# Three rooms and two score banks in PSUM for three attention stages, with q, k and x turned split as they leave PSUM

## The chip, the cores and the metric

One core of one Trainium2 chip runs the whole program. The time is that of the device, in microseconds, and lower is better. The engines are TensorE (PE in the rows; PEld are its weight loads), VectorE (DVE), ScalarE (ACT), GpSimd (POOL) and SyncE (SP), which issues most transfers. SBUF is the memory of 128 partitions from which the engines work; PSUM, into which TensorE writes, has 8 banks of 128 x 512 floats.

## The reference

Eight layers are added to x (8 samples of 256 tokens, width 256) one after the other, each scaled by a gate. The change touches three attentions, with 16 heads of width 16:

```python
# l1x: cross attention on ctx_768, masked queries attend to all keys alike
q = x @ Wq.T; k, v = y @ Wkv.T
attn = softmax(where(pad_mask, (q * scale) @ k, -1e9)); out = attn @ v
...
# l3x: cross attention with biases and a clip
q = query @ Wq + bq; k = key_value @ Wk + bk; v = key_value @ Wv + bv
attn = softmax(clip(q @ k * scale, -CLAMP, CLAMP)); out = (attn @ v) @ Wo + bo
...
# l3f: self attention under two key masks; five register tokens see both
qkv = x @ W_qkv; x_pos, x_neg = masked_attn(pos), masked_attn(~pos)
out = concatenate([(x_pos[:REG] + x_neg[:REG]) * 0.5, where(pos, x_pos, x_neg)]) @ W_proj + b_proj
```

x enters each layer normalized. The other layers are a similarity, a feed-forward layer, two mixtures of experts and an attention of another kind.

## The kernel before

The program is written engine by engine; each engine runs its list in order and waits on semaphores. Nine phases follow each other: l0x, l0f, l1x, l1f, l2x, l2f, l3x, sim, l3f. l1x, l3x and l3f are instances of `Packed` and run through the functions `packing`, one for each engine. This order is written out by hand: a loop over n (a sample) and in it over the 16 heads h, in which `if h == ...` places the other work of samples n − 1 to n + 3.

Products of q, k, v and their inputs are taken in three passes over a high and a low part of each operand (`mm3`). For this each tensor is split: high is the value rounded to the fast format, low the rest. Before, xT (x normalized and transposed) and k are copied out of PSUM by ScalarE (`turned`, `keys`, into xt and kf), q by VectorE (`queries`, into qf, with mask or bias), and then GpSimd makes both parts (`parts`: a cast, L719, and a subtraction, L721). SyncE copies the parts of q and k into qpack and kpack (L572), so that a head's scores are one matmul of 48 rows.

For each head TensorE makes the scores (`scores`, L2012), VectorE takes their negated maximum (`maximum`, L1080), and TensorE makes them a second time, transposed and with the maximum folded in as two more rows (`scores_turned`, L2029); ScalarE writes the exponential (L1619), in l3x VectorE clips it (L1172), and `values` multiplies it by v (L2044). The maxima of 8 heads are turned by TensorE (m0 and m1, L1998) and go into qpack by a transfer. The outputs are turned (z0 and z1, L2054), divided by their sums on VectorE (L1152 and L1159), in l1x added to x (L903), in l3x and l3f turned again ("on", L2066 to L2071) and projected ("y", L2079). l3f has beside this attention of its registers: us, ut and up (L2088, L2096, L2104).

PSUM: scores use the banks 0, 1 and 5 in turn, the transposed ones 2 and 3, the values 4. All else takes two rooms, the banks 6 and 7, in turn, in an order that `Packed` lists. TensorE waits before each use until the use two before it has been released:

```python
def room(self, what, n):
    b = sum(self.used) % 2
    self.place[what, n] = b, self.used[b]
...
if i >= 3:
    pe.wait_ge(m["mx"], at["mx"] + i - 2)
```

## Time and profile before

| | |
|---|---|
| median of three runs | 2746.6 us (2744.47 to 2755.7) |
| profiled execution: time, span | 2744.37 us, 2742.6 us |
| mean granted TensorE clock, share of full | 0.827 |
| PE, DVE, ACT, POOL busy | 77%, 47%, 27%, 33% of the span |
| l1x, l3x, l3f | about 264 to 502, 2082 to 2361, 2435 to 2735 us |

An engine's busy time is the union of its instructions. A wait is idle time just before an instruction, put down to what released it last. The granted clock is a share of 2.4 GHz, where 0.5 is 1.2 GHz. A room's release is seen only through what released it: TensorE at L1998 waiting for "DVE x L903" is m0 waiting for a room that the addition to x frees.

### The profile page before, as it was taken

Reading aid. Unit: us, or ns where it says so; the run is one execution under the profiler, and the core shown is the slowest. Engines: PE = TensorE matmul, PEld = TensorE weight load, DVE = VectorE, ACT = ScalarE, POOL = GpSimd, SP = SyncE. Lnnn points to the kernel's source line nnn. Section 1 sums busy time; section 2 is a strip of 40 time slices with the busy share of each in tenths; the row PEclk is TensorE's granted clock in tenths of the full one; section 3 lists DMA queues with packets and bytes.
Section 4 is the critical chain, followed back from the end, with each engine's and each line's share of the span. In section 5 each row is a group of like instructions: output and inputs, shape, how many; then the busy total and the mean of one; then the engine's idle time right before and its main releaser. Section 6 shows DMA issues by size and latency. Waiting matters only on the chain.

```text
span 2742.6 us, 32575 instructions
## 1 busy us (share of the span) xinstructions
PE 2110.3 (77%) x11634; PEld 1555.5 (57%) x11634; DVE 1292.8 (47%) x2652; ACT 729.5 (27%) x1621; POOL 896.9 (33%) x822
## 2 busy tenths in 40 slices
PE   3597888529999981788988899569953988549887
PEld 3476655427777771455655566458842655335554
DVE  2444566525454442233334334535534798445554
ACT  1121245202221110223332333112310344112344
...
GB/s 128 156 162 5 86 75 49 66 92 104 125 115 96 123 81 106 63 4 3 3 0 3 3 3 0 6 71 107 202 80 81 59 67 35 0 26 61 49 50 45
DMA packets 120208, 177.73 MB, mean 65 GB/s; under 512 B 10900, under 2 KB 105172, under 8 KB 117460
## 3 DMA queue, kind: packets, MB, share of 16 engines
...
q14 instruction: 49, 0.40, 0.1%
...
## 4 chain that ended last, share of the span: by engine, by line
PE 52%; issue 18%; DVE 11%; POOL 8%; DMA 5%; ACT 3%; SPq 1%; another core or an unknown queue 1%; DVEq 0%; POOLq 0%; ACTq 0%
PE bank L1735 8%; PE bank L1736 6%; PE bank L1737 6%; PE bank L1859 5%; PE bank L2012 4%; PE bank L1838 4%; PE bank L2044 4%; DMA ew<-in_we 3%; POOL ewl L773 3%; PE bank L1872 3%; PE bank L1886 3%; DVE nmf L1080 2%; PE bank L1849 2%; DVE x L1356 1%; POOL ewh L771 1%
## 5 line engine op out<-in xcount | busy, mean ns | idle before, releaser
L1080 DVE TENSOR_REDUCE nmf<-bank 128x2 f32<-128x512 f32 x384 | 258.9, 688 | 200.8 <-PE bank L2012 199.3
L1619 ACT ACTIVATE pT<-bank 128x512 f32<-128x512 f32 x384 | 223.2, 597 | 350.5 <-PE bank L2029 348.9
L1328 DVE TENSOR_TENSOR bank<-sil,bank 128x512 f32<-128x512 f32 x136 | 94.8, 697 | 312.7 <-ACT sil L1669 300.6
L1735 PE MATMUL bank<-split,ewl 128*128 128x512 f32 x514 | 213.4, 415 | 34.1 <-POOL ewl L773 17.3
L2012 PE MATMUL bank<-kpack,qpack 48*128 48x256 f32 (+1 forms) x768 | 201.6, 372 | 25.6 <-DMA qpack<-qhl 15.6
L2029 PE MATMUL bank<-qpack,kpack 50*128 50x256 f32 (+1 forms) x768 | 201.6, 364 | 12.7 <-ACT pT L1619 12.7
L773 POOL TENSOR_TENSOR ewl<-ew,ewh 128x1536 fp32r<-128x1536 f32 (+1 forms) x47 | 205.9, 4381 | 3.8
L1736 PE MATMUL bank<-split,ewh 128*128 128x512 f32 x514 | 204.5, 398 | 0.0
L1737 PE MATMUL bank<-split,ewh 128*128 128x512 f32 x514 | 204.3, 397 | 0.0
L771 POOL CAST ewh<-ew 128x1536 fp32r<-128x1536 f32 (+1 forms) x47 | 85.3, 1814 | 354.6 <-DMA ew<-in_we 343.9
L1002 DVE TENSOR_REDUCE nmax<-bank 128x2 f32<-128x512 f32 x128 | 87.6, 690 | 233.4 <-PE bank L1859 230.1
L838 POOL TENSOR_TENSOR esum<-esum,minus 128x2 f32<-128x2 f32 x128 | 89.8, 702 | 327.6 <-ACT arena L1528 327.5
L2012 PEld LDWEIGHTS bank<-kpack,qpack 48*128 48x128 f32 (+1 forms) x768 | 130.8, 226 | 110.0 <-issue 49.8
L1528 ACT ACTIVATE arena<-bank,nmax 128x256 f32<-128x256 f32 x256 | 118.9, 470 | 248.1 <-DVE nmax L1002 246.0
L1735 PE MATMUL bank<-ewh,split 128*128 128x256 f32 x544 | 168.1, 309 | 19.6 <-DVE split L1331 13.1
L1669 ACT ACTIVATE sil<-bank 128x512 f32<-128x512 f32 x136 | 81.3, 598 | 352.4 <-PE bank L1737 319.5
L1462 ACT ACTIVATE arena<-bank 128x512 f32<-128x512 f32 x154 | 91.9, 597 | 300.4 <-PE bank L1838 112.6
L1859 PE MATMUL bank<-arena 64*128 64x256 f32 x512 | 155.9, 447 | 6.2 <-ACT arena L1462 6.2
L1736 PE MATMUL bank<-ewl,split 128*128 128x256 f32 x544 | 156.7, 288 | 0.0
L1737 PE MATMUL bank<-ewh,split 128*128 128x256 f32 x544 | 156.1, 287 | 0.0
L2029 PEld LDWEIGHTS bank<-qpack,kpack 50*128 50x128 f32 (+1 forms) x768 | 127.1, 216 | 29.8 <-ACT pT L1619 18.9
L1735 PEld LDWEIGHTS bank<-split,ewl 128*128 128x128 f32 x514 | 98.4, 191 | 73.9 <-DVE split L1331 21.0
...
## 6 DMA issues: line engine op xcount, KB each, us to landing
...
```

The lines of the kernel that those rows point to most:

```text
L771: nc.gpsimd.tensor_copy(high, whole).then_inc(m["wh"], 1)
L773: nc.gpsimd.tensor_tensor(low, whole, high, ALU.subtract).then_inc(m["ws"], 1)
L1080: V.tensor_reduce(nmf[:, c, :, j, r], bank[(0, 1, 5)[i % 3]][:, :].rearrange("p (t k) -> p t k", t=T), AXX, ALU.max, negate=True).then_inc ...
L1528: ins = A(prob[h % 3][:, t * S:(t + 1) * S], bank[h % 3][:, t * S:(t + 1) * S], ACT.Exp, bias=nmax[:, h, t:t + 1], accum_out=esum[:, h, t: ...
L1619: A(pT16[i % 8][:, :], bank[2 + h % 2][:, :], ACT.Exp, scale=s.qscale).then_inc(m["e"], 1)
L1735: mm(out_, al, bh, start=start, stop=False)
L1736: mm(out_, ah, bl, start=False, stop=False)
L1737: return mm(out_, ah, bh, start=False, stop=stop)
L1838: ins = mm(dst, w[:, c, gr * P:(gr + 1) * P], of[:, c, :], start=c == 0, stop=c == kt_ - 1)
L1859: ins = mm(bank[h % 3][:, t * S:(t + 1) * S], qT[0][r0:r0 + 64, gr, t * P:(t + 1) * P], kT[r0:r0 + 64, gr, :], start=True, stop=True)
L2012: ins = mm(bank[(0, 1, 5)[i % 3]][:, t * S:(t + 1) * S], q[rows, r, t * P:(t + 1) * P], k[rows, r, :], start=True, stop=True)
L2029: ins = mm(bank[2 + h % 2][:, t * S:(t + 1) * S], k[rows, r, t * P:(t + 1) * P], q[rows, r, :], start=True, stop=True)
```

## The change

The three stages get three rooms (banks 5, 6 and 7) and two score banks (0 and 1). The high part of xT, k and q is now written by ScalarE straight out of PSUM, with the bias where there is one (`high_part`, `turned`), and the low part by VectorE, which subtracts the high part from the same bank and then frees the room by a memset that waits for the subtraction (`low_part`). GpSimd keeps the split of the context and the power for the norm. q has two split buffers. In l1x the mask is a factor on rstd in place of one on q, and the two halves of a sample are added to x in one operation. In l3x the bias of v is multiplied by wo once and added to the output's bias. The register scores of l3f take the split parts in three passes. Several pieces of work move by one to four heads.

```diff
+        self.banks, self.rooms = (0, 1), (5, 6, 7)
...
-        self.place, self.used = {}, [0, 0]
+        self.place, self.used = {}, [0 for _ in self.rooms]
...
+        if bias:
+            self.room("bt", 0)
+            self.room("by", 0)
         for n in range(-3, B + 1):
-            for what, at, there in (("us", n + 2, own), ("m1", n, True), ("v", n + 2, True), ("xT", n + 3, True),
-                                    ("ut", n + 2, own), ("z0", n - 1, True), ("z1", n - 1, True), ("up", n + 2, own),
+            for what, at, there in (("us", n + 2, own), ("m1", n, True), ("v", n + 2, True), ("ut", n + 2, own),
+                                    ("z0", n - 1, True), ("z1", n - 1, True), ("xT", n + 3, True), ("up", n + 2, own),
                                     ("m0", n + 1, True), ("on", n - 1, self.proj), ("k", n + 3, True),
                                     ("q", n + 3, True), ("y", n - 1, self.proj)):
...
-        b = sum(self.used) % 2
+        b = sum(self.used) % len(self.rooms)
...
+                        sp.wait_ge(m["ks"], at["ks"] + p + 1)
+                        rows_of(0, kpack[p % 3], khl, (0, 0, 1), m[f"kl{p % 3}"])
...
+                        sp.wait_ge(m["qs"], at["qs"] + p + 1)
                         for j in range(2):
-                            rows_of(p, j, qpack[p % 3], qhl, (0, 1, 0))
+                            rows_of(j, qpack[p % 3], qhl[p % 2], (0, 1, 0), m[f"pl{p % 3}"])
...
-                def parts(dst, src, done, k):
-                    nc.gpsimd.tensor_copy(dst[:, 0, :, :], src).then_inc(m[done], 1)
-                    pool.wait_ge(m[done], at[done] + 2 * k + 1)
-                    nc.gpsimd.tensor_tensor(dst[:, 1, :, :], src, dst[:, 0, :, :], ALU.subtract).then_inc(m[done], 1)
...
-                                used("q", p - 1)
-                                used("v" if s.own else "q", p - 1)
-                            parts(xT16, xt[:, :, :], "xs", p)
...
-                            filled("k", p)
-                            if p > 0:
-                                sent(p - 1)
-                            parts(khl, kf[:, :, :], "ks", p)
...
+                    if p < B and not s.own:
+                        pool.wait_ge(m["ct"], at["ct"] + 16 * p + 16)
+                        if p > 0:
+                            used("v", p - 1)
+                        nc.gpsimd.tensor_copy(cT16[:, 0, :, :], ct[:, :, :]).then_inc(m["cs"], 1)
+                        pool.wait_ge(m["cs"], at["cs"] + 2 * p + 1)
+                        nc.gpsimd.tensor_tensor(cT16[:, 1, :, :], ct[:, :, :], cT16[:, 0, :, :], ALU.subtract)\
+                            .then_inc(m["cs"], 1)
+                    if p + 1 < B:
+                        root({"asked": asked[s.name]}, p + 2, rstd[:, :], rstd[:, :], mhalf[:, 0:T])
...
+                    if s.mask:
+                        ch.link(tt(rstd[:, :], rstd[:, :], maskf[:, n * T:(n + 1) * T], ALU.mult))
...
+                def low_part(what, n, hl, bias=None):
+
...
+                    dve.wait_ge(m[sent], at[sent] + n + 1)
+                    if what == "xT":
+                        if n > 0:
+                            made("q", n - 1)
+                            made("v" if s.own else "q", n - 1)
+                    elif what == "k" and n > 0:
+                        dve.wait_ge(m[f"kl{(n - 1) % 3}"], at[f"kl{(n - 1) % 3}"] + 96 * ((n - 1) // 3 + 1))
+                    elif what == "q" and n > 1:
+                        dve.wait_ge(m[f"pl{(n - 2) % 3}"], at[f"pl{(n - 2) % 3}"] + s.packs * ((n - 2) // 3 + 1))
+                    if what == "k" and s.own and n > 0:
+                        made("us", n - 1)
...
+                    if what == "q" and s.own:
...
+                        ch.link(tt(whole, src[:, :, 0:NREG].rearrange("p j (r o) -> p j r o", o=1).broadcast_to(four),
+                                   hm[:, :, :].rearrange("p j (o h) -> p j o h", o=1).broadcast_to(four), ALU.mult))
+                        ch.link(V.tensor_copy(qx[:, 0, :, :], qxf[:, :, :]))
+                        tt(qx[:, 1, :, :], qxf[:, :, :], qx[:, 0, :, :], ALU.subtract).then_inc(m["ux"], 1)
+                    high, low = hl[:, 0, :, :], hl[:, 1, :, :]
+                    if bias is None:
+                        tt(low, src, high, ALU.subtract).then_inc(m[parts], 1)
...
+                        for j in range(2):
+                            ins = stt(low[:, j, :], src[:, j, :], bias[:, j:j + 1], high[:, j, :], ALU.add, ALU.subtract)
+                        ins.then_inc(m[parts], 1)
+                    dve.wait_ge(m[parts], at[parts] + n + 1)
+                    V.memset(idle[:, 1:2], 0.0).then_inc(done, 1)
...
+                        tt(both[:, t * D:(t + 1) * D].rearrange("p (h e) -> p h e", h=NH), z4[:, :, 0:16], scale, ALU.mult)\
+                            .then_inc(done, 1)
+                        if t == T - 1:
+                            for u in range(T):
+                                b, k = s.place[f"z{u}", n]
+                                dve.wait_ge(m[f"mf{b}"], at[f"mf{b}"] + k + 1)
+                            ch.link(stt(x[:, n * T:(n + 1) * T, :], both[:, :].rearrange("p (t d) -> p t d", t=T), gate,
+                                        x[:, n * T:(n + 1) * T, :], ALU.mult, ALU.add))
...
+                        if h == 0 and 0 <= n + 2 < B:
+                            low_part("q", n + 2, qhl[n % 2], bq3 if s.bias else None)
...
-                        if h == 5 and s.bias and 0 <= n + 2 < B:
-                            values(n + 2)
...
-                        if h in (7, 8) and 0 <= n - 1 < B:
-                            outputs(n - 1, h - 7)
...
+                        if h == 6 and 0 <= n - 1 < B:
+                            outputs(n - 1, 0)
+                        if h == 8 and 0 <= n - 1 < B:
+                            outputs(n - 1, 1)
+                        if h == 9 and n + 3 < B:
+                            low_part("xT", n + 3, xT16)
...
+                        if h == 13 and n + 3 < B:
+                            low_part("k", n + 3, khl, bk3 if s.bias else None)
...
-                        if h == 14 and n + 3 < B:
-                            queries(n + 3)
-                            if s.own:
-                                register_queries(n + 3)
...
+                    from_, _ = made("xT", n)
...
-                    copy(xt[:, :, :], halves(from_)).then_inc(done, 1)
...
+                    copy(xT16[:, 0, :, :], halves(from_)).then_inc(m["xh"], 1)
...
+                        act.wait_ge(m[f"kl{(n - 1) % 3}"], at[f"kl{(n - 1) % 3}"] + 96 * ((n - 1) // 3 + 1))
+                    if what == "q" and n > 1:
+                        act.wait_ge(m[f"pl{(n - 2) % 3}"], at[f"pl{(n - 2) % 3}"] + s.packs * ((n - 2) // 3 + 1))
+                    if bias is None:
+                        ins = copy(hl[:, 0, :, :], halves(from_))
+                    else:
                         for j in range(2):
-                            ins = A(kf[:, j, :], from_[:, j * S:(j + 1) * S], ACT.Identity, bias=bk3[:, j:j + 1])
...
-                    ins.then_inc(done, 1)
+                            ins = A(hl[:, 0, j, :], from_[:, j * S:(j + 1) * S], ACT.Identity, bias=bias[:, j:j + 1])
+                    ins.then_inc(m[what + "h"], 1)
...
-                        if h == 6 and n + 3 < B:
-                            turned(n + 3)
...
+                        if h == 9 and n + 3 < B:
+                            turned(n + 3)
...
-                        if h == 12 and n + 3 < B:
-                            keys(n + 3)
+                        if h == 13 and n + 3 < B:
+                            high_part("k", n + 3, khl, bk3 if s.bias else None)
+                        if h == 15 and n + 3 < B:
+                            high_part("q", n + 3, qhl[(n + 3) % 2], bq3 if s.bias else None)
...
-                    if i >= 3:
-                        pe.wait_ge(m["mx"], at["mx"] + i - 2)
+                    if i >= len(s.banks):
+                        pe.wait_ge(m["mx"], at["mx"] + i + 1 - len(s.banks))
...
-                        mm(to[0:NX, 0:S], qx[:, j, :], kf[:, j, :], start=j == 0, stop=False)
+                        mm3(to[0:NX, 0:S], [qx[:, w, j, :] for w in range(2)], [khl[:, w, j, :] for w in range(2)], j == 0, False)
...
-                        if h == 0 and s.own and 0 <= n + 2 < B:
+                        if h == 0 and s.proj and 0 <= n - 2:
+                            projected(n - 2, 1)
...
-                        if h == 5 and n + 3 < B:
+                        if h == 4 and s.own and 0 <= n + 2 < B:
+                            register_turned(n + 2)
+                        if h == 5 and 0 <= n - 1:
+                            outputs(n - 1, 0)
+                        if h in (6, 10, 14) and 0 <= n < B:
+                            values(n, h // 4 - 1)
+                        if h == 7 and 0 <= n - 1:
+                            outputs(n - 1, 1)
+                        if h == 8 and n + 3 < B:
                             turned(n + 3)
...
-                            outputs(n - 1, h - 6)
-                        if h in (5 + s.late, 9 + s.late, 13 + s.late) and 0 <= n < B:
-                            values(n, h // 4 - 1)
...
-                        if h == 9 and 0 <= n + 1 < B:
+                        if h == 10 and 0 <= n + 1 < B:
                             maxima(n + 1, 0)
...
-                        if h in (10, 11) and n + 3 < B:
-                            keys(n + 3, h - 10)
-                        if h in (12, 13) and n + 3 < B:
-                            queries(n + 3, h - 12)
-                        if h in (14, 15) and s.proj and 0 <= n - 1:
-                            projected(n - 1, h - 14)
+                        if h in (11, 12) and n + 3 < B:
+                            keys(n + 3, h - 11)
+                        if h in (13, 14) and n + 3 < B:
+                            queries(n + 3, h - 13)
```

What stands on TensorE in l1x, for a sample in the middle of the stage, from the first turning of outputs (L2054) on. L2012 are scores, L2029 the transposed ones; the names show the banks. Before:

```order
L2012 MATMUL bank0<-kpack0,qpack0 128x256 x2
L2029 MATMUL bank2<-qpack2,kpack2 128x256 x2
L2054 MATMUL bank7<-ident,oT16 128x128 x4
L2012 MATMUL bank1<-kpack0,qpack0 128x256 x2
L2029 MATMUL bank3<-qpack2,kpack2 128x256 x2
L2054 MATMUL bank6<-ident,oT16 128x128 x4
L2012 MATMUL bank5<-kpack0,qpack0 128x256 x2
L2029 MATMUL bank2<-qpack2,kpack2 128x256 x2
L2012 MATMUL bank0<-kpack0,qpack0 128x256 x2
L2029 MATMUL bank3<-qpack2,kpack2 128x256 x2
```

And in the changed kernel, where L2016, L2033, L2058 and L1967 are scores, transposed scores, outputs turned and x turned:

```order
L2016 MATMUL bank1<-kpack0,qpack0 128x256 x2
L2033 MATMUL bank3<-qpack2,kpack2 128x256 x2
L2058 MATMUL bank7<-ident,oT16 128x128 x4
L2016 MATMUL bank0<-kpack0,qpack0 128x256 x2
L2033 MATMUL bank2<-qpack2,kpack2 128x256 x2
L1967 MATMUL bank5<-ident,xn 128x128 x4
L2016 MATMUL bank1<-kpack0,qpack0 128x256 x2
L2033 MATMUL bank3<-qpack2,kpack2 128x256 x2
L2016 MATMUL bank0<-kpack0,qpack0 128x256 x2
L2033 MATMUL bank2<-qpack2,kpack2 128x256 x2
```

Scores alternate between two banks instead of three, x is turned behind both outputs instead of ahead of them, and the rooms are three.

On VectorE in l1x, the reductions (L1080) with what stands between them, from one sample's z0 to the statistics of a later sample. Before:

```order
L1149 RECIPROCAL recs<-bank 128x16
L1152 TENSOR_TENSOR scr<-bank,recs 128x256
L903 SCALAR_TENSOR_TENSOR x<-scr,tgx,x 128x256
L1080 TENSOR_REDUCE nmf<-bank 128x2
L1149 RECIPROCAL recs<-bank 128x16
L1152 TENSOR_TENSOR scr<-bank,recs 128x256
L903 SCALAR_TENSOR_TENSOR x<-scr,tgx,x 128x256
L1080 TENSOR_REDUCE nmf<-bank 128x2 x2
L1061 BN_STATS bst<-x 128x6 x2
L1064 BN_AGGR mv<-bst 128x2 x2
L1066 TENSOR_SCALAR rstd<-mv 128x2
L1080 TENSOR_REDUCE nmf<-bank 128x2 x3
```

In the changed kernel (L1062 are the reductions, L1106 and L1112 the low part and the memset that frees the room):

```order
L1134 RECIPROCAL recs<-bank 128x16
L1137 TENSOR_TENSOR both<-bank,recs 128x256
L1062 TENSOR_REDUCE nmf<-bank 128x2
L1076 CAST nmhl<-nmf 128x4x4
L1077 TENSOR_TENSOR nmhl<-nmf,nmhl 128x4x4
L1062 TENSOR_REDUCE nmf<-bank 128x2
L1134 RECIPROCAL recs<-bank 128x16
L1137 TENSOR_TENSOR both<-bank,recs 128x256
L1143 SCALAR_TENSOR_TENSOR x<-both,tgx,x 128x512
L1062 TENSOR_REDUCE nmf<-bank 128x2
L1106 TENSOR_TENSOR xT<-bank,xT 128x512
L1112 MEMSET idle 128x1
```

One addition for both halves stands where two stood, and the low part of xT with its memset comes behind it; those of k and q follow further down, where a copy of q stood.

On VectorE in l3x, around the place where q is taken, with the clips (L1172, now L1163). Before:

```order
L1073 TENSOR_SCALAR xn<-x,mv,rstd 128x256 x2
L1172 TENSOR_SCALAR pT_5<-pT_5 128x512
L1080 TENSOR_REDUCE nmf<-bank 128x2
L1106 TENSOR_TENSOR qf<-bank,bq 128x512
L1172 TENSOR_SCALAR pT_6<-pT_6 128x512
L1080 TENSOR_REDUCE nmf<-bank 128x2
L1090 TENSOR_SCALAR nmf<-nmf 128x16
L1091 TENSOR_SCALAR nmf<-nmf 128x16
L1094 CAST nmhl<-nmf 128x4x4
L1095 TENSOR_TENSOR nmhl<-nmf,nmhl 128x4x4
```

In the changed kernel:

```order
L1062 TENSOR_REDUCE nmf<-bank 128x2
L1163 TENSOR_SCALAR pT_4<-pT_4 128x512
L1062 TENSOR_REDUCE nmf<-bank 128x2
L1109 SCALAR_TENSOR_TENSOR khl<-bank,bk,khl 128x256 x2
L1112 MEMSET idle 128x1
L1163 TENSOR_SCALAR pT_5<-pT_5 128x512
L1062 TENSOR_REDUCE nmf<-bank 128x2
L1055 TENSOR_SCALAR xn<-x,mv,rstd 128x256 x2
L1163 TENSOR_SCALAR pT_6<-pT_6 128x512
L1062 TENSOR_REDUCE nmf<-bank 128x2
L1072 TENSOR_SCALAR nmf<-nmf 128x16
L1073 TENSOR_SCALAR nmf<-nmf 128x16
```

The low part of k with its bias has come in, ahead of the norm; q's follows behind the maxima.

## Rows read from the trace of the kernel before

**Rows 1.** windows: us; busy PE, PEld, DVE, ACT, POOL; PEclk, DMA share, GB/s
```profile
315.60:441.90 126.30, 112.61 (x874) 74.92 (x874) 83.81 (x158) 59.56 (x114) 40.59 (x44) 0.81 0.47 68
2134.50:2276.50 142.00, 124.61 (x909) 80.79 (x910) 120.15 (x260) 60.49 (x117) 41.56 (x44) 0.79 0.43 61
2522.20:2660.70 138.50, 120.04 (x829) 75.90 (x830) 75.26 (x152) 53.64 (x105) 25.33 (x27) 0.80 0.29 49
```

**Rows 2.** waits of PE in l1x: us in total, times, longest
```profile
PE bank L2012 <- DVE nmf L1080: 5.0, 11, 1.2
PE bank L1998 <- DVE x L903: 4.2, 6, 1.0
PE bank L1735 <- DVE x L903: 3.7, 4, 0.9
```

**Rows 3.** waits of PE in l3x (2100 to 2350)
```profile
PE bank L2054 <- DVE v L1141: 6.9, 3, 2.3
PE bank L1998 <- DVE on L1159: 5.8, 5, 2.0
PE bank L2012 <- DVE nmf L1080: 4.3, 13, 0.4
```

**Rows 4.** waits of PE in l3f (2435 to 2743)
```profile
PE bank L1735 <- ACT pu L1594: 9.4, 6, 1.6
PE bank L2054 <- ACT xt L1462: 5.2, 4, 1.3
PE bank L2104 <- DVE on L1159: 5.0, 5, 1.2
PE bank L2096 <- ACT v L1462: 2.7, 5, 0.7
```

**Rows 5.** timeline of PE (start, us), and windows, in l1x
```profile
405.39 0.38 PE L1998 MATMUL bank<-ident,nmhl 128*16 128x128 f32 x2 [0.93 <-DVE x L903]
407.14 0.36 PE L1735 MATMUL bank<-cT,wks 96*128 96x256 f32 x1 [0.93 <-DVE x L903]
...
403.00:409.00 6.00, 4.13 (x43) 2.68 (x42) 5.83 (x14) 2.82 (x6) 1.06 (x1) 0.97 1.06 114
409.00:416.00 7.00, 7.00 (x43) 4.63 (x42) 2.92 (x8) 1.88 (x4) 2.58 (x3) 0.54 0.12 32
```

**Rows 6.** groups on DVE in l3x, then their min/median/max ns
```profile
L1172 DVE TENSOR_SCALAR pT<-pT 128x512 f32<-128x512 f32 x128 | 59.7, 467 | 12.0 <-ACT pT L1619 11.3
L1090 DVE TENSOR_SCALAR nmf<-nmf 128x16 f32<-128x16 f32 x16 | 7.7, 480 | 0.6
...
L1172 DVE TENSOR_SCALAR pT<-pT x128: 408/419/1375, 2138.2 to 2345.6; 128x512 f32<-128x512 f32 x128
L1090 DVE TENSOR_SCALAR nmf<-nmf x16: 174/176/1222, 2122.0 to 2324.4; 128x16 f32<-128x16 f32 x16
```

**Rows 7.** waits of DVE in l3x, 2134.5 to 2276.5
```profile
DVE nmf L1080 <- PE bank L2012: 20.0, 24, 2.5
```

**Rows 8.** groups in l1x: busy us, mean ns, idle before
```profile
L903 DVE SCALAR_TENSOR_TENSOR x<-scr,tgx,x 128x256 f32<-128x256 f32 x16 | 7.8, 485 | 0.6
L1103 DVE TENSOR_TENSOR qf<-bank,mask_u 128x512 f32<-128x512 f32 x8 | 5.5, 684 | 4.5 <-PE bank L1737 4.5
L1462 ACT ACTIVATE xt<-bank 128x512 f32<-128x512 f32 x8 | 4.7, 594 | 20.0 <-PE bank L1964 20.0
```

**Rows 9.** timeline of DVE: two operations in l3x, a memset in l0f
```profile
2248.89 0.68 DVE L1080 TENSOR_REDUCE nmf<-bank 128x2 f32<-128x512 f32 x1
2249.49 0.68 DVE L1106 TENSOR_TENSOR qf<-bank,bq 128x512 f32<-128x512 f32 x1
...
258.45 0.06 DVE L955 MEMSET idle<- 128x1 f32 x1
```

**Rows 10.** timeline of POOL, first k of l1x
```profile
276.51 0.61 POOL L719 CAST khl<-kf 128x512 fp32r<-128x512 f32 x1 [1.11 <-ACT kf L1462]
277.20 1.28 POOL L721 TENSOR_TENSOR khl<-kf,khl 128x512 fp32r<-128x512 f32 x1
```

206 lines of the change are left out of this document (87 added, 119 removed).

## The prediction

> **What bounds the kernel now.** The change touches three of nine stages, so I began with the windows by stage. Each window in [rows 1] runs from one write of qf (q, copied out of PSUM) to the fifth after it (fourth in l3f), so a sample takes 126.3/5 = 25.3 us in l1x, 142.0/5 = 28.4 in l3x and 138.5/4 = 34.6 in l3f. The reader should see two things there. TensorE is busy 89%, 88% and 87%, at a mean granted clock of 0.81, 0.79 and 0.80: with only the levels 1.2 and 2.4 GHz that is the low one for about 40% of the time. VectorE is busy 66%, 85% and 54%: l3x is nearly bound by it, the others are not.
>
> Next the waits of TensorE. Those on rooms (a bank used in turn by all that is not scores) are, over whole stages: l1x, the score maxima m0 wait for z0 and k waits for z1, 4.2 + 3.7 [rows 2]; l3x, z0 for v and m0 for z0, 6.9 + 5.8 [rows 3]; l3f, v for us, z0 for xT, up for z0 and ut for v, 9.4 + 5.2 + 5.0 + 2.7 = 22.3 [rows 4]. Waits on score banks are small with three of them: 5.0 and 4.3 us in l1x and l3x [rows 2, 3].
>
> Last, what follows such waits. In one sample of l1x TensorE stands 0.93 us twice, at 405.4 and 407.1; in 403 to 409 it has the clock 0.97, and in the 7 us after it 0.54 while it is busy all the time and VectorE only 2.92 us [rows 5]. So the waits may cost more than they last.
>
> **The change, part by part.** The profiled execution took 2744.4 us (span 2742.6); the median of the three runs is 2.2 above it.
>
> *Rooms.* A use of a room now waits for the use three before it, not two, and the order written out gives the release and the next use more heads of distance (z0 at head 5 and its division at 6, m0 at 10; before 6, 7 and 9). In l1x the room is also free after the division, not after the addition to x. I take all of the waits named: −(7.9 + 12.7 + 22.3) = −42.9. From above the bound is this; from below half of it, −21, since rooms of xT, k and q are now held until VectorE has made the low part.
>
> *Clock.* If the low clock were gone, the third of the work done at it would take half: (1 − 0.81)/0.5 × 126.3/2 = 24.0 us in l1x, 0.40 × 138.5/2 = 27.7 in l3f. In l3x VectorE would not follow, so nothing. Bounds 0 and −52; I take a third, −17, because the only removed cause I see in a row is the pair of waits in [rows 5], and prologues are at the low clock as well.
>
> *Splits.* GpSimd made high and low of xT, k and q; each pair took 0.61 + 1.28 us after a copy by another engine [rows 10]. Now ScalarE writes the high part (0.594, like its copy, [rows 8]) and VectorE subtracts out of PSUM (0.684, as the other 128x512 operation with a PSUM operand; with a bias two of 128x256 at 0.485 [rows 8]), and a memset frees the room. At the start of a stage the first k goes out 1.28 + 0.61 − 0.68 = 1.2 us earlier: −3.7 for three stages. ScalarE has an operation more per sample (in l3x two more), against 60 busy of 126 to 142 [rows 1]: hidden.
>
> *VectorE's load.* Per sample in l1x: three subtractions 2.05 come, one masked copy 0.68 and, with the two additions merged into one, about 0.2 go. In l3x 0.68 + 4 × 0.485 = 2.62 come and two PSUM operations of the 0.68 kind (q, v) go. Also gone is most of what GpSimd costs VectorE: the clip of l3x has a median of 419 ns and a mean of 467, the operation at line 1090 176 and 480, with single ones above 1.2 us [rows 6]: 59.7 − 128 × 0.419 = 6.1 and 7.7 − 16 × 0.176 = 4.9, together 11 us in the stage or 1.4 per sample. I take three quarters of it, as three of GpSimd's four subtractions go (the context's stays). So l3x: 24.0 + 2.6 − 1.4 − 1.0 = 24.2 per sample, plus the releases. VectorE still has room: 20.0 us of its idle time in that window was waiting for scores [rows 7], 4.0 per sample.
>
> *Releases.* A reduction of 0.68 us is followed by the next operation after 0.60 [rows 9]; the wait before the memset ends that overlap, 0.08 + 0.06 = 0.14 us, three times in 24 samples, 10 us on VectorE. On the path only in l3x: +3.4. The Trainium skill (VectorE: DVE Perf Modes, The DRAIN you can't avoid) says that no operation starts before the pipe is empty and that a semaphore costs nothing extra. By that rule it would be the memset alone, 0.06, and +1.4. The trace disagrees: 0.60 is less than 0.68.
>
> *VectorE waits for ScalarE.* The low part needs the high part, which stands behind an exponential. Both start when their matmul ends: 0.6 + 0.6 on ScalarE against 0.69 on VectorE, 0.5 us, three times in 8 samples of l3x is 12; 0 if VectorE lags. I take +4. What queues behind it is the next head's reduction, and for that TensorE waits two heads later.
>
> *Two score banks.* Scores i wait for the reduction of i − 2, not i − 3. No row has two. Below, 0: a sample has 16 heads in 25 us, so a reduction is due in two periods of 1.6, and needs 0.7. Above, 384 heads × 0.1. With three banks it was 9.8 us [rows 2, 3] (l3f 0.5); I take twice, +10. In l3f the room of "on" now waits for VectorE's low xT: +0.5 × 8 = +4.
>
> *At nothing:* the bias of v taken through wo (two transposes, two matmuls, a copy, an addition, once) lies beside the load and GpSimd's split of the first context, without which k can't start; uncovered it is 3 us, from two operations of 0.6 and matmuls of 0.4. The mask as a factor on two columns of rstd, 0.17 us, is a copy of q less. Register scores as three products of the fast kind instead of one slow one, the tiles in w13, k and q on separate semaphores: the same rows are sent by the same 12 transfers (16 in l3f) in the same place of SyncE's queue, k's waits only become looser. GpSimd's powers no longer stand behind splits.
>
> **Sum:** 2744.4 − 42.9 − 17 − 3.7 + 3.4 + 4 + 10 + 4 = 2702, against the median 2704.
>
> **The rivals.**
> *The forecast:* rooms free in time, some clock back, 2675 to 2725. For it: VectorE's slack in [rows 1], and that TensorE's room waits name a release each.
> *The clock comes back in whole:* 2704 − 35 = 2669, with no new bank waits 2655. For it: 7 us at 0.54 directly behind two short waits [rows 5]. Against: heads 5 to 10 of l1x ask VectorE for 6 reductions of 0.69, the low xT, the merged addition and two divisions, some 7 us, and TensorE at the high clock for less, so new short waits arise.
> *The waits change their name:* TensorE waits for reductions with two banks where it waited for rooms. Then no clock is gained and a quarter of the room waits comes back too, beside the new terms of 3.4 + 4 + 10 + 4: 2746.6 − 32 − 4 + 21 = 2732. For it: VectorE is busy 5.83 of 6 us in 403 to 409 [rows 5]. The Trainium skill (TensorE: Matmul & The Clock Gate, A second HAM failure mode: psum-queue depth-cycling) says that cycling through PSUM banks makes TensorE idle briefly so often that the clock oscillates. By that rule the clock term is 0, whatever the rooms do: 2721. The trace agrees as far as two waits of 0.93 go.
> *Slower:* the two banks stop TensorE in every group of bare heads. It decides when the bank waits pass 43 + 17 + 4 = 64 us, 2.7 per sample, which is three waits of 0.93; at four, 3.7 × 24 = 89, no clock gained: 2746.6 − 43 − 4 + 89 = 2789, milder 2765. Against: with one bank more they were 0.4 per sample.
>
> **How the numbers follow.** Forecast 0.50; whole clock 0.15; waits renamed 0.25, half of it beyond 0.5% faster; slower 0.10. A measurement of this kernel tells about 0.5%, 13.7 us, from no change. So faster 0.77, same 0.13, slower 0.10. The likeliest case has 2675 to 2725; the range takes in most of the clock and of the renamed waits: 2655 to 2742.
>
> **What would show it.** In the profile after: the waits of TensorE for z0, z1, v, us and xT gone from l1x, l3x and l3f; waits for the reduction below 25 us in all; samples of about 23, 26.5 and 31 us; clips with a mean near 430 ns; VectorE's idle time before the low parts, put down to ScalarE, below 15 us in l3x; the clock of the three windows 0.83 or more. Wrong would make it: bank waits of several tenths at each head, low parts that hold the reductions back, or a clock that falls as before although the room waits are gone.

## The result and the profile after

The changed kernel takes 2664.7 us (median of four, 2651.4 to 2670.8) where the kernel before takes 2751.0 in the same comparison (2744.5 to 2755.7): a ratio of 0.968, interval 0.964 to 0.973. That is 86 us less. The prediction was 2704, so 42 less. The direction is right and the time lies in the range of 2655 to 2742, but the gain is twice what was forecast: it lies outside the likeliest case (2675 to 2725) and beside the rival "the clock comes back in whole" (2669), which had a chance of 0.15.

The profiled execution of the changed kernel is its fastest (span 2649.7 us, 92.9 less than before). Windows over the whole of the three stages, first before, then after (columns as in [rows 1]):

```profile
264.30:502.20 237.90, 198.21 (x1440) 132.80 (x1440) 141.83 (x290) 97.26 (x184) 65.63 (x72) 0.74 0.43 62
2082.30:2360.70 278.40, 223.83 (x1536) 147.08 (x1536) 201.92 (x458) 100.87 (x193) 66.72 (x72) 0.76 0.37 53
2435.10:2734.60 299.50, 253.33 (x1684) 162.81 (x1684) 154.12 (x324) 109.02 (x210) 51.77 (x56) 0.79 0.29 46
```

```profile
267.50:486.70 219.20, 184.99 (x1440) 123.37 (x1440) 142.22 (x332) 101.18 (x192) 20.55 (x24) 0.79 0.49 67
2053.20:2314.60 261.40, 220.85 (x1542) 143.31 (x1542) 199.64 (x506) 112.08 (x218) 21.10 (x24) 0.77 0.42 57
2390.30:2641.70 251.40, 218.12 (x1700) 144.87 (x1700) 158.88 (x381) 114.00 (x218) 5.57 (x8) 0.90 0.36 55
```

l1x takes 18.7 us less, l3x 17.0, l3f 48.1; the remaining 9 are in stages whose code didn't change. TensorE's time has two parts. Idle (the window less PE busy) was 39.7, 54.6 and 46.2 before and is 34.2, 40.6 and 33.3 after, 32.4 less in all. Busy, with the same matmuls but for a few, was 675.4 before and is 624.0 after: 13.2 less in l1x, 3.0 in l3x and 35.2 in l3f. The 51.4 us of the second are put down to the clock. The reader can check it in l3f: 0.79 of full speed over 299.5 us is 126 us at the lower of the two levels, 0.90 over 251.4 is 50, and half of the 76 us between them is 38; busy time fell by 35.

The clock does not rise evenly. These are two windows of the changed kernel, one in l1x and one in l3f, cut where the granted clock changes:

```profile
346.90:445.80 98.90, 89.71 (x876) 58.12 (x872) 80.52 (x178) 62.33 (x119) 9.63 (x11) 1.00 0.66 89
2480.20:2627.00 146.80, 140.87 (x1245) 91.68 (x1248) 104.86 (x239) 85.20 (x164) 2.07 (x3) 1.00 0.35 56
```

99 us and 147 us without a fall. In the kernel before, read in steps of 1 us, no stretch at the high clock in l1x lasted longer than 17 us, and it fell in every sample, as in [rows 5]; in l3f its longest was 62.

TensorE's waits in the changed kernel, in l1x, in l3x and (two rows) in l3f:

```profile
PE bank L2016 <- DVE nmf L1062: 12.2, 27, 0.8
...
PE bank L2016 <- DVE nmf L1062: 17.1, 26, 1.3
...
PE bank L1738 <- DVE qx L1103: 6.8, 8, 1.8
PE bank L2016 <- DVE nmf L1062: 4.4, 7, 0.9
```

The waits of [rows 2 to 4] for rooms (released by x, v, pu, xt and on) are gone. The register scores of l3f (through `mm3`, L1738) wait 6.8 us for their own operand qx, 3.1 before. Waits for reductions have grown from 9.8 us in all to 33.7.

The release takes as long as [rows 9] made one expect. In VectorE's timeline the operation behind a reduction starts 0.60 us after it, the one behind a low part (L1106) 0.72 us after it, and the memset (L1112) lies beside that next operation:

```profile
368.19 0.69 DVE L1062 TENSOR_REDUCE nmf<-bank 128x2 f32<-128x512 f32 x1
368.79 0.68 DVE L1106 TENSOR_TENSOR qhl<-bank,qhl 128x512 fp32r<-128x512 f32 x1
369.51 0.69 DVE L1062 TENSOR_REDUCE nmf<-bank 128x2 f32<-128x512 f32 x1
369.54 0.06 DVE L1112 MEMSET idle<- 128x1 f32 x1
```

### The profile page after: what moved, and what is told of

Read it like the earlier page. It is cut to its first block, busy times and chain, and to the rows that moved or that the text cites. A ratio compares the mean times of both kernels' runs of the same rounds, so it can differ in the third digit from the quotient of the medians.

```text
span 2649.7 us, 32700 instructions
## 1 busy us (share of the span) xinstructions
PE 2047.9 (77%) x11656; PEld 1518.4 (57%) x11656; DVE 1295.5 (49%) x2798; ACT 749.6 (28%) x1662; POOL 760.1 (29%) x678
## 4 chain that ended last, share of the span: by engine, by line
PE 53%; issue 18%; DVE 10%; POOL 9%; DMA 5%; ACT 2%; SPq 1%; another core or an unknown queue 1%; DVEq 0%; POOLq 0%; ACTq 0%
PE bank L1738 8%; PE bank L1739 6%; PE bank L1740 6%; PE bank L2016 5%; PE bank L1862 5%; PE bank L1841 4%; PE bank L2048 3%; DMA ew<-in_we 3%; POOL ewl L753 3%; PE bank L1875 3%; PE bank L1889 3%; DVE nmf L1062 2%; PE bank L1852 2%; POOL arena L779 2%; POOL ewh L751 1%
## 5 line engine op out<-in xcount | busy, mean ns | idle before, releaser
L1062 DVE TENSOR_REDUCE nmf<-bank 128x2 f32<-128x512 f32 x384 | 261.0, 689 | 122.7 <-PE bank L2016 120.1
L1738 PE MATMUL bank<-split,ewl 128*128 128x512 f32 x514 | 213.2, 415 | 47.5 <-DVE split L1324 29.8
L2016 PE MATMUL bank<-kpack,qpack 48*128 48x256 f32 (+1 forms) x768 | 205.5, 370 | 56.8 <-DVE nmf L1062 33.7
L2016 PEld LDWEIGHTS bank<-kpack,qpack 48*128 48x128 f32 (+1 forms) x768 | 128.8, 219 | 142.5 <-DVE nmf L1062 72.9
L2033 PE MATMUL bank<-qpack,kpack 50*128 50x256 f32 (+1 forms) x768 | 196.3, 352 | 6.7 <-ACT pT L1617 6.4
L1738 PE MATMUL bank<-ewh,split 128*128 128x256 f32 x544 | 166.0, 305 | 6.5 <-issue 6.5
L707 POOL TENSOR_TENSOR rstd<-rstd,mhalf 128x2 f32<-128x2 f32 x40 | 28.4, 709 | 431.6 <-DVE rstd L1046 241.5
L1738 PEld LDWEIGHTS bank<-split,ewl 128*128 128x128 f32 x514 | 98.5, 192 | 87.1 <-DVE split L1324 26.9
```

Of the source, the lines that this page charges most:

```text
L1062: V.tensor_reduce(nmf[:, c, :, j, r], bank[s.banks[i % len(s.banks)]][:, :] .rearrange("p (t k) -> p t k", t=T), AXX, ALU.max, negate=True ...
L1738: mm(out_, al, bh, start=start, stop=False)
L2016: ins = mm(bank[s.banks[i % len(s.banks)]][:, t * S:(t + 1) * S], q[rows, r, t * P:(t + 1) * P], k[rows, r, :], start=True, stop=True)
L2033: ins = mm(bank[2 + h % 2][:, t * S:(t + 1) * S], k[rows, r, t * P:(t + 1) * P], q[rows, r, :], start=True, stop=True)
```

## The experiments

All are compared with the kernel before on the same chip; a chip's kernel before took 2722 to 2751 us, so ratios are compared across groups and not times. The stages, whose lengths in us are the last three columns, are read from one profiled execution each. That of before is the fastest of its four (2744.4 of 2744.4 to 2755.7), so differences from its stages may be on the small side: e3's stages add up to 11 us less where its median is 26 less, e8's to 35 where its median is 57 less.

| kernel | median us (before) | ratio, interval | l1x | l3x | l3f |
|---|---|---|---|---|---|
| before | | | 237.9 | 278.4 | 299.5 |
| changed | 2664.7 (2751.0) | 0.968, 0.964 to 0.973 | 219.2 | 261.4 | 251.4 |
| e6: changed, again | 2637.5 (2730.2) | 0.966, 0.961 to 0.970 | 230.7 | 263.2 | 258.7 |
| e1: two rooms, three banks | 2633.8 (2725.0) | 0.966, 0.963 to 0.969 | 223.6 | 246.2 | 276.1 |
| e2: two rooms, two banks | 2657.5 (2725.0) | 0.976, 0.973 to 0.980 | 224.1 | 260.0 | 274.7 |
| e3: before, three rooms | 2699.4 (2725.0) | 0.991, 0.987 to 0.995 | 251.8 | 289.8 | 263.5 |
| e4: GpSimd's load back | 2674.2 (2725.0) | 0.977, 0.972 to 0.982 | 227.3 | 291.3 | 261.8 |
| e8: before, small splits | 2673.6 (2730.2) | 0.980, 0.975 to 0.984 | 217.4 | 256.8 | 306.4 |
| e9: e3 and e8 | 2676.1 (2750.7) | 0.976, 0.972 to 0.980 | 226.8 | 269.6 | 258.3 |
| e7: l3x three banks | 2625.5 (2730.2) | 0.962, 0.958 to 0.967 | 230.7 | 257.3 | 254.9 |
| e5: direct release | 2634.0 (2730.2) | 0.967, 0.962 to 0.971 | 217.8 | 257.1 | 259.9 |
| e10: stops that weren't | 2665.5 (2750.7) | 0.970, 0.967 to 0.972 | 224.6 | 258.1 | 258.6 |
| e11: combined | 2653.1 (2750.7) | 0.966, 0.963 to 0.969 | 212.4 | 245.8 | 256.2 |
| e12: stops for reductions | 2672.7 (2721.5) | 0.980, 0.977 to 0.984 | 224.6 | 260.1 | 290.5 |

How much one stage scatters can be read where its code is the same: l1x 219.2, 230.7, 230.7, 224.6 and 224.6 (changed, e6, e7, e10, e12), l3x 261.4, 263.2, 258.1 and 260.1, l3f 251.4, 258.7, 254.9 and 258.6. So a difference below some 12 us in l1x or 7 in the others says nothing here.

**The first group** asked which part of the change brings the gain. The theory after the result was the third room: it takes the waits for rooms away, and so gives the clock back. The rival was the split.

e1, in the changed kernel:

```diff
-        self.banks, self.rooms = (0, 1), (5, 6, 7)
+        self.banks, self.rooms = (0, 1, 5), (6, 7)
```

> The changed kernel (2665 us) with the old two rooms and three score banks in all three stages; the early split by ScalarE and VectorE and the new order stay. Rooms theory (the third room takes TensorE's waits for rooms away, and without them TensorE keeps the high clock for a hundred us on end, which is the larger half of the gain): both come back, 2735 to 2765, with waits for rooms of 35 us or more in all, and no stretch at the high clock over 50 us in l1x and l3f. Split theory (the gain is from the splits: GpSimd no longer slows VectorE, and parts are ready earlier): 2690 or less, since the split is untouched.

Measured: 0.966, the same as the changed kernel. The rooms theory falls for the whole: with two rooms the new order leaves some 25 us of waits for rooms (by their releasers), and still l1x keeps the high clock for 105 us on end and l3f for 89. Trading a score bank for a room is worth nothing on the whole. By stage the theory holds in one: l3f is worse without the third room, and l3x is better with the third score bank:

```profile
262.60:486.20 223.60, 195.01 (x1440) 129.81 (x1440) 141.70 (x331) 101.12 (x192) 20.56 (x24) 0.74 0.49 66
2028.70:2274.90 246.20, 207.21 (x1542) 138.49 (x1542) 197.63 (x509) 111.30 (x218) 21.43 (x24) 0.81 0.43 60
2351.00:2627.10 276.10, 236.83 (x1700) 157.27 (x1700) 159.62 (x380) 113.50 (x218) 5.55 (x8) 0.82 0.33 50
```

e2 leaves bank 5 unused:

```diff
-        self.banks, self.rooms = (0, 1), (5, 6, 7)
+        self.banks, self.rooms = (0, 1), (6, 7)
```

> The changed kernel with two rooms (6 and 7) and two score banks, bank 5 unused. Against e1 it prices the third score bank alone, against the changed kernel the third room alone. Prediction's term for two banks was +10: e1 plus 10 to 25 us, 2750 to 2785 by the rooms theory. If score banks cost nothing: equal to e1 within 6. Split theory: 2700 or less.

Measured: 0.976; the intervals of e1 and e2 don't touch. So with two rooms the third score bank is worth 24 us (2657.5 less 2633.8). Of these the profiled executions show 13, all of it in l3x (14); in l1x and l3f there is nothing beyond scatter:

```profile
263.00:487.10 224.10, 188.64 (x1440) 123.41 (x1440) 143.23 (x330) 101.35 (x192) 20.57 (x24) 0.77 0.48 66
2029.30:2289.30 260.00, 215.80 (x1542) 140.24 (x1542) 199.74 (x507) 111.86 (x218) 21.22 (x24) 0.80 0.41 57
2365.10:2639.80 274.70, 234.83 (x1700) 155.22 (x1700) 160.28 (x381) 113.84 (x218) 5.56 (x8) 0.83 0.33 50
```

Against the changed kernel e2 prices the third room: nothing in l1x and l3x, 16 to 23 us in l3f, the only stage in which the register attention (us, ut and up) uses rooms too.

e3 gives the kernel before the rooms and banks of the changed one and nothing else:

```diff
-        self.place, self.used = {}, [0, 0]
+        self.place, self.used = {}, [0, 0, 0]
...
-        b = sum(self.used) % 2
+        b = sum(self.used) % 3
...
-                    return bank[6 + b], m[f"mf{b}"]
+                    return bank[5 + b], m[f"mf{b}"]
...
-                    if i >= 3:
-                        pe.wait_ge(m["mx"], at["mx"] + i - 2)
+                    if i >= 2:
+                        pe.wait_ge(m["mx"], at["mx"] + i - 1)
```

> The kernel before with three rooms (5, 6, 7) and two score banks; its order, its copies and GpSimd's splits are untouched. Rooms theory: most of the gain is here already, 2680 to 2710, with waits for rooms below 15 us and long stretches at the high clock in l1x and l3f. Split theory: 2735 to 2755, since GpSimd works as before. By the two-bank term alone it would lose 10 us.

Measured: 0.991, 26 us less. The time lies where the rooms theory put it only because this chip's kernel before takes 2725; it is less than a third of the gain, not most of it. l3f gains 36 us, and l1x and l3x lose 14 and 11:

```profile
263.70:515.50 251.80, 211.72 (x1440) 136.91 (x1440) 144.01 (x292) 97.78 (x184) 65.52 (x72) 0.69 0.41 59
2066.50:2356.30 289.80, 232.53 (x1536) 151.93 (x1536) 195.44 (x459) 100.74 (x193) 66.68 (x72) 0.73 0.35 51
2429.40:2692.90 263.50, 234.65 (x1684) 151.37 (x1684) 156.89 (x325) 107.91 (x210) 51.72 (x56) 0.85 0.33 52
```

TensorE's waits for reductions have grown, in l1x, l3x and l3f. Before they were 5.0, 4.3 and 0.5:

```profile
PE bank L2012 <- DVE nmf L1080: 19.1, 29, 1.4
...
PE bank L2012 <- DVE nmf L1080: 26.6, 32, 2.1
...
PE bank L2012 <- DVE nmf L1080: 5.7, 9, 0.9
```

The waits for rooms in l1x and l3x, 20.6 us, are gone as foreseen, and 36.4 us of waits for score banks have come. That is the rival "the waits change their name", true in two stages of three. But the waits alone don't make these two longer: TensorE's idle time is 40.1 and 57.3 us where it was 39.7 and 54.6, and the rest of the loss, 13.5 and 8.7 us, is busy time, at clocks of 0.69 and 0.73 for 0.74 and 0.76. In l1x the loss of 14 is little more than the scatter. Of l3f's 36 us, 17.3 are idle time and 18.7 busy time.

e4, in the changed kernel, on GpSimd, beside each of the three high parts:

```diff
+                            pool.wait_ge(m[what], at[what] + p + 1)
+                            nc.gpsimd.tensor_copy(junk[:, :], src).then_inc(m["jk"], 1)
+                            pool.wait_ge(m["jk"], at["jk"] + j + 1)
+                            nc.gpsimd.tensor_tensor(junk[:, :], src, junk[:, :], ALU.subtract).then_inc(m["jk"], 1)
```

> The changed kernel with GpSimd's old load put back as idle work: three pairs of a 128x512 copy and subtraction per sample in each of the three stages, on a tile of their own, that nothing waits for but GpSimd's own next power. It prices what GpSimd costs the others while it works. The prediction gave 1.0 us per sample on VectorE in l3x, 8 us on the path: 2670 to 2675. Rooms theory: below +10, GpSimd is no large part. Split theory: +30 or more, 2695.

Measured: 0.977 against 0.966 to 0.970 for the changed kernel, about 1% or 20 to 30 us where the prediction's price was 8, and l3x 28 to 33 us longer:

```profile
2034.00:2325.30 291.30, 248.93 (x1542) 160.44 (x1542) 219.41 (x507) 112.38 (x218) 66.06 (x72) 0.67 0.37 51
```

The clips (here L1176, in the changed kernel L1163) show the contact. First with the load, then without:

```profile
L1176 DVE TENSOR_SCALAR pT<-pT 128x512 f32<-128x512 f32 x128 | 66.5, 520 | 7.7 <-ACT pT L1630 6.6
```

```profile
L1163 DVE TENSOR_SCALAR pT<-pT 128x512 f32<-128x512 f32 x128 | 56.9, 445 | 6.4 <-ACT pT L1617 5.3
```

VectorE is busy 19.8 us more in l3x (219.4 for 199.6) with the same operations, half of it in the clips; operations that read PSUM keep their times (reductions 687 ns in both, the low part of k 479 for 478). TensorE's idle time is 42.4 us for 40.6; what makes the stage longer is its busy time, 248.9 for 220.9, at a clock of 0.67 for 0.77. VectorE's waits for GpSimd's power are 0.9 us with the load and without it, so what is priced is contention. In l1x and l3f the load costs nothing beyond scatter. In l1x it doesn't meet the operation on the maxima that e8 below is about, which keeps 174 to 177 ns.

**The second group** asked for GpSimd's price in the kernel before, the additions by stage, and the release.

> The changed kernel itself once more, as the mark for the others of this group and to see how much its stages scatter. Its four times went from 2651 to 2671. Expected 2640 to 2665 beside a kernel before of about 2725 if this is the chip of e1 to e4; the three stages within 5 us of 219, 261 and 251. If the long stretch at the high clock in l3f (147 us) was luck of one execution, l3f will be nearer 275.

Measured: see the table; the long stretch in l3f returned (123 us), but l1x took 11.5 us more and l3f 7.3, both outside the 5 us expected.

e8, in the kernel before:

```diff
+                    c = slice(0, S if k == 0 or done == "cs" else 8)
-                    nc.gpsimd.tensor_copy(dst[:, 0, :, :], src).then_inc(m[done], 1)
+                    nc.gpsimd.tensor_copy(dst[:, 0, :, c], src[:, :, c]).then_inc(m[done], 1)
```

and the subtraction likewise. The kernel leaves out most of the parts of seven samples, so only its time is of use.

> The kernel before, in which GpSimd makes the parts of xT, k and q in full for the first sample of a stage only, and for the other seven only 16 of 512 columns (so q, k and v of those samples are left out of the result). Order, rooms, banks, copies and waits are those of before. It prices what GpSimd's splits cost the kernel before, by contention and by their latency. By the prediction (1.0 us per sample on VectorE, and nothing else): 8 to 12 us less than before, all in l3x. By e4, where putting the load back took 30 us in l3x, 8 in l1x and 10 in l3f: 35 to 50 us less, most of it in l3x. If e4's price came only from where its load stands: below 15.

Measured: 0.980, 57 us less than before. The prediction had given GpSimd's hold on VectorE 8 us, all in l3x. By stage it is about 20 us in l1x (where 12 can be scatter) and 22 in l3x; in l3f it is nothing:

```profile
265.70:483.10 217.40, 185.17 (x1440) 124.26 (x1440) 129.62 (x292) 96.80 (x184) 35.20 (x72) 0.78 0.49 68
2030.20:2287.00 256.80, 209.36 (x1536) 139.26 (x1536) 187.04 (x460) 100.87 (x193) 37.43 (x72) 0.81 0.41 58
2361.40:2667.80 306.40, 262.36 (x1684) 167.45 (x1684) 144.37 (x324) 108.76 (x210) 20.99 (x56) 0.75 0.28 45
```

How they cost is best seen in l1x of the kernel before. L1095 subtracts 16 columns, and takes 174 ns or 1.2 us; nine of its 16 executions are at the upper end (the group, then its min/median/max ns):

```profile
L1095 DVE TENSOR_TENSOR nmhl<-nmf,nmhl 128x16 fp32r<-128x16 f32 x16 | 12.3, 766 | 0.6
...
L1095 DVE TENSOR_TENSOR nmhl<-nmf,nmhl x16: 174/1214/1242, 304.2 to 476.7; 128x16 fp32r<-128x16 f32 x16
```

Two of them on VectorE, and the subtractions (L721) that GpSimd made at the time:

```profile
418.64 1.22 DVE L1095 TENSOR_TENSOR nmhl<-nmf,nmhl 128x16 fp32r<-128x16 f32 x1
427.71 1.24 DVE L1095 TENSOR_TENSOR nmhl<-nmf,nmhl 128x16 fp32r<-128x16 f32 x1
```

```profile
418.56 1.27 POOL L721 TENSOR_TENSOR qhl<-qf,qhl 128x512 fp32r<-128x512 f32 x1
427.62 1.29 POOL L721 TENSOR_TENSOR xT<-xt,xT 128x512 fp32r<-128x512 f32 x1
```

VectorE's short operation starts while GpSimd's is under way and ends with it: 418.64 + 1.22 = 419.86 beside 418.56 + 1.27 = 419.83, and 428.95 beside 428.91. It is no chance meeting. GpSimd splits q as soon as VectorE has copied it, and a head later VectorE makes these maxima: that is six of the nine, in each sample from 317 to 443 us; the other three meet the split of xT. In the changed kernel all take 174 to 177 ns in the three stages, and in e8's l1x, where GpSimd's operations are short, 174 to 182:

```profile
L1097 DVE TENSOR_TENSOR nmhl<-nmf,nmhl x16: 174/175/182, 305.1 to 457.5; 128x16 fp32r<-128x16 f32 x16
```

The Trainium skill (SBUF — State Buffer, SBUF: two separate sides) says that VectorE and GpSimd share a pair of ports as an exclusive lock, and that the one that comes second waits for the whole of the other's instruction; for VectorE this holds in its two-port modes and, against a GpSimd instruction that reads SBUF, with two inputs in SBUF. The trace agrees for the second: L1095 has two inputs in SBUF. For the first it only speaks: the clip has one input, and does 512 elements from SBUF in 0.42 us where an operation on PSUM takes 0.68; which mode it ran in no run shows. The reductions, which read PSUM, have means of 687 to 689 ns in all kernels. e8 takes away the lock and also GpSimd's latency, so its price is for both together; in l1x VectorE was busy 12.2 us less (129.6 for 141.8). Over the three stages TensorE was idle 16.8 us less and busy 18.4 us less.

The longest stretches at the high clock separate the two causes by stage. In l1x e8 has 105 us (328.5 to 433.5) with the old order and two rooms, and e3, with the third room, 26. In l3f e3 has 139.5 us, and e8 64, as before:

```profile
328.50:433.50 105.00, 96.76 (x936) 64.76 (x934) 78.58 (x171) 63.69 (x124) 17.08 (x42) 1.00 0.63 87
```

```profile
2503.50:2643.00 139.50, 135.43 (x1160) 86.97 (x1156) 109.46 (x214) 75.18 (x148) 31.94 (x34) 1.00 0.41 67
```

e9 is e3 with the edit of e8.

> e3 and e8 in one: the kernel before, three rooms and two score banks, and GpSimd's parts of xT, k and q in full only for the first sample of a stage and 16 of 512 columns for the others (left out of the result). If the two gains add by stage and the two score banks cost what they cost in e3 (l1x +14, l3x +11): l1x 231, l3x 268, l3f 270, about 2663. If the two banks only cost while GpSimd holds VectorE up: waits for reductions fall from 51 us to 25 or less, l1x 217, l3x 257 and l3f 263 to 270, about 2640 to 2650, which is what the changed kernel takes.

Measured:

```profile
263.40:490.20 226.80, 190.03 (x1440) 125.77 (x1440) 131.18 (x291) 97.61 (x184) 34.87 (x72) 0.77 0.46 65
2062.80:2332.40 269.60, 214.77 (x1536) 140.73 (x1536) 188.64 (x460) 100.60 (x193) 36.77 (x72) 0.78 0.39 55
2406.60:2664.90 258.30, 230.52 (x1684) 150.17 (x1684) 144.14 (x325) 108.13 (x210) 21.02 (x56) 0.85 0.34 53
```

By stage the gains come near the first of the two expectations: 226.8 and 269.6 for 231 and 268, and l3f better still. On the whole they don't add: 0.976 where the product of e3 and e8 would be 0.970, with an interval that overlaps e8's. Two score banks cost l3x 13 us over e8 although GpSimd is out of the way (in l1x 9, within scatter), and TensorE's waits for reductions are 45 us in all, so the second expectation falls. The third room gives l3f 48 us over e8.

e7 gives l3x alone the banks and rooms of e1.

```diff
-        self.banks, self.rooms = (0, 1), (5, 6, 7)
+        self.banks, self.rooms = ((0, 1, 5), (6, 7)) if clip else ((0, 1), (5, 6, 7))
```

> The changed kernel with two rooms and three score banks in l3x alone; l1x and l3f keep three rooms and two score banks. Theory from e1 and e2 (stages add up: l3x wants the third score bank, l3f the third room): l3x 246, l1x 219, l3f 251, so 12 to 16 us less than the changed kernel and faster than e1. Rival (the stages' gains are scatter of the clock): no difference beyond 5 us.

Measured: 12 us below e6 in the medians, with intervals that overlap, and l3x 257.3 where the theory had 246. TensorE's waits for reductions in l3x fell from 18 to 4 us as in e1. Inconclusive on the time.

e5 releases by the subtraction:

```diff
-                        tt(low, src, high, ALU.subtract).then_inc(m[parts], 1)
+                        tt(low, src, high, ALU.subtract).then_inc(done, 1)
...
-                    dve.wait_ge(m[parts], at[parts] + n + 1)
-                    V.memset(idle[:, 1:2], 0.0).then_inc(done, 1)
```

> The changed kernel with the low part's subtraction itself freeing the room; who waited for the part now waits for the room's release, and the wait on VectorE and the memset, 24 times, are gone. By the prediction's price of 0.14 us each, on the path in l3x only: 3.4 us less than e6. By the page's rule (only the memset, 0.06): 1.4. If a release's delay counts for TensorE's waits and clock too: 6 to 12 less.

Measured: 3.5 us below e6, far inside the scatter. VectorE was busy 2.4, 2.1 and 1.9 us less than in e6 in the three stages, and the next reduction starts 0.60 us after a low part again. Neither price on the path can be told apart.

**The third group** asked whether stops cost more than they last, and for the sum of what helped.

e10, in the changed kernel:

```diff
-                        pe.wait_ge(m["e"], at["e"] + i - 1)
+                        pe.wait_ge(m["e"], at["e"] + i - 1 + (1 if s.own and h in (4, 12) else 0))
```

> The changed kernel; in l3f TensorE waits at heads 4 and 12 of each sample for the exponential of the head just before, so it stands twice per sample for an exponential's 0.6 us, and no work is added. If a stop costs what it lasts: 16 x 0.6 = 10 us in l3f, 261 to 268. If stops also take the high clock away: 275 to 300, with the low clock for 100 us or more where it had 61 to 78, and no stretch at the high clock over 60 us.

Measured: no stop came. TensorE waited 1.9 us for exponentials in l3f, as in the changed kernel, since the exponential is always done by then. It tests nothing and stands as one more execution of the changed kernel.

e12 puts the wait where it bites:

```diff
                             scores(n + 1, h)
+                            if s.own and h in (4, 12):
+                                pe.wait_ge(m["mx"], at["mx"] + (n + 1) * NH + h + 1)
```

> The changed kernel; in l3f TensorE waits at heads 4 and 12 of each sample until the reduction of the scores it has just made is done, 0.69 us and a start each, so 16 stops of 0.8 to 1.0 us, 13 to 16 us in all, and no work is added. e10 had no stops, since its wait was always over. If a stop costs what it lasts: l3f 267 to 275 where it was 251 to 260. If stops also take the high clock away: 285 to 305, with the low clock for 120 us or more where it had 61 to 85, and no stretch at the high clock over 50 us.

Measured, the wait and the stage:

```profile
PE bank L2033 <- DVE nmf L1062: 11.5, 14, 1.3
```

```profile
2373.60:2664.10 290.50, 247.43 (x1700) 162.64 (x1700) 159.65 (x380) 113.99 (x218) 5.55 (x8) 0.81 0.31 47
```

For comparison the changed kernel in e6, where the last row is l3f:

```profile
264.50:495.20 230.70, 198.90 (x1440) 130.15 (x1440) 142.21 (x332) 101.24 (x192) 20.54 (x24) 0.71 0.47 64
2041.10:2304.30 263.20, 220.96 (x1542) 142.89 (x1542) 199.75 (x509) 112.00 (x218) 21.07 (x24) 0.77 0.41 56
2380.40:2639.10 258.70, 226.17 (x1700) 150.64 (x1700) 159.28 (x380) 113.94 (x218) 5.56 (x8) 0.85 0.35 53
```

14 stops, 11.5 us in all, make l3f 290.5 instead of 251 to 259. TensorE is idle 10.5 us more than in e6 and busy 21.3 us more, with the same 1700 matmuls, at a clock of 0.81 for 0.85. A stop of 0.8 us in this stage costs 2.3 to 2.8. The whole kernel agrees: its ratio is 0.980 where the changed kernel has 0.966 to 0.968. Of the expectation only the stage's length came as foreseen. The low clock lasted 110 us (0.19/0.5 × 290.5) and not 120 or more, and a high stretch of 106 us was left in the stage's second half where none over 50 was expected.

e11 joins e5 and e7 and moves the register work of l3f:

```diff
-                        if h == 1 and s.own and 0 <= n + 2 < B:
+                        if h == 2 and s.own and 0 <= n + 2 < B:
                             register_scores(n + 2)
```

and so for its maximum, exponential and turning, each one head later.

> The changed kernel with all that helped: three score banks and two rooms in l3x (e7), the release by the subtraction itself (e5), and in l3f the register scores, their maximum, exponential and turning one head later, so that TensorE no longer waits 6.8 us for qx. If they add: 0.9623 and 0.1% and 0.3% less, a ratio of 0.957 to 0.960 and 2612 to 2622 where before is 2730. If the register work only moves the wait on: equal to e7, 0.962.

Measured: 0.966; 12 us below e10 on the same chip, with intervals that overlap. Its profile has the shortest l1x of all and an l3x as in e1:

```profile
265.90:478.30 212.40, 178.14 (x1440) 119.08 (x1440) 139.69 (x306) 101.22 (x192) 20.55 (x24) 0.82 0.52 70
2051.60:2297.40 245.80, 206.29 (x1542) 137.94 (x1542) 195.68 (x483) 111.11 (x218) 21.18 (x24) 0.82 0.43 60
2371.80:2628.00 256.20, 227.79 (x1700) 151.70 (x1700) 156.85 (x356) 113.12 (x218) 5.57 (x8) 0.85 0.35 54
```

The wait for qx fell from 6.8 to 2.5 us and l3f did not get shorter. The expected 0.957 to 0.960 did not come. e11 is the best candidate but is not shown to be faster than the changed kernel.

## Why the prediction was right and where it failed

Take the 92.9 us of the profiles as the sum does. All its terms but the clock's are −42.9 − 3.7 + 3.4 + 4 + 10 + 4 = −25.2; TensorE's idle time fell by 32.4. The clock's is −17; busy time fell by 51.4. The other 9.1 lie in stages that it left alone. So the main term that was mis-sized is the clock's. That the others come out near is in part luck: the rooms gave less than their term in two stages, the score banks cost more, and against that stood GpSimd's splits, which are in no term of the sum and whose end took 16.8 us of idle time away in e8.

*Rooms (−42.9).* All named waits went, as said. As a gain of its own the term was right only in l3f, and there too small: e3 gives 36 us and e9 48 for 22.3 of waits, with half of e3's gain in busy time. In l1x and l3x the 20.6 us were paid back (e3).

*Two score banks (+10).* Mis-sized. Measured +23.9 us of waits in the changed kernel, and +41.6 in the old order (e3); in time 24 us between e1 and e2. The step that failed is the doubling of a row with three banks, "With three banks it was 9.8 us ... I take twice". One bank less leaves one period of scores between a reduction and the next use of its bank, and what VectorE does between two reductions shows in waits of up to 1.3 us.

*GpSimd's load on VectorE (−1.0 per sample, l3x alone).* This step failed too. The price was worked out from two rows of l3x [rows 6], none of l1x was used, and nothing of it went into the sum. The row that was missed in l1x, L1095 with a mean of 766 ns, cost 9.5 us of VectorE's time (12.3 less 16 × 0.174) and stood just ahead of TensorE's maxima. e8 measures about 20 us in l1x and 22 in l3x where the term has 0 and 8. e4 confirms l3x from the other side; for l1x it says nothing, as its load doesn't meet L1095.

*Clock (−17, bounds 0 and −52).* It gave 51.4. The bound was no bound: it was worked out over windows of five samples in l1x and four in l3f, not the eight of a stage, and l3f alone gave 35.2 where it allows 27.7. The step "I take a third, because the only removed cause I see in a row is the pair of waits" counted one cause of several: GpSimd's hold on VectorE was another (e8's 18.4 us of busy time), and e12 shows that stops of 0.8 us at two heads of a sample cost 21.3 us of busy time. The argument of [rows 5], that the fall stands behind the stops, was right. The claim that l3x would get nothing was nearly right (PE busy 3.0 us less). By the Trainium skill (TensorE: Matmul & The Clock Gate, A second HAM failure mode: psum-queue depth-cycling), which tells of another kernel whose clock oscillates because TensorE idles briefly as it cycles through banks, this term would have been 0. Cycling by itself does not do it here: the changed kernel takes its banks in turn at every head and kept the full clock for 147 us. That short idling costs clock agrees with e12 (0.81 for 0.85).

*Releases (+3.4).* The duration was right: 0.12 us for 0.14. What it does to the time lies below the scatter (e5). The Trainium skill (VectorE: DVE Perf Modes, The DRAIN you can't avoid) says that a semaphore costs nothing extra; by the prediction's reading it would have been the memset alone, 0.06. The trace disagrees: the next operation starts 0.72 us after a low part with the wait and 0.60 after it without (e5), and the memset lies beside it. The same section says that a next operation that is not held starts earlier, which the prediction left out; the 0.60 behind a reduction of 0.68 agrees with that.

*Waits for ScalarE (+4).* VectorE's waits for ScalarE's high parts in l3x are 13.7 us, below the 15 named, and 5.3 of them are one wait. What they cost on the path no run tells.

*Splits (−3.7).* Didn't come. The first scores start 0.8 us earlier after the start of l1x and of l3x than before, and 1.2 later in l3f.

*What would show it.* Room waits gone: yes. Waits for reductions below 25 us: no, 33.7. Samples of 23, 26.5 and 31 us: 21.7, 25.6 and 25.6 over the same five and four samples. Clips near 430 ns: 445. Clock of 0.83 or more in these windows: yes, 0.88, 0.85 and 0.97.

Of the 93 us of the profiles, the runs give the end of GpSimd's splits some 40 (e8, l1x and l3x), the third room in l3f 16 to 48, depending on the order around it (e2, e3, e9), and the loss of the third score bank costs l3x up to 14. These don't add up: e1, with the old rooms and banks, is as fast as the changed kernel, so the trade that the change is named after is not what made it faster. What e1 has over before, the split, the order and the smaller parts of the change, is enough. What the new order by itself does in l3f, where e1 with two rooms is 23 us below before while e8 shows no gain from GpSimd, was not separated from the early split, and stays open. So do the 9 us in stages with unchanged code; l1f and l2x scatter by 6 and 8 us over all profiled executions.
